# Two feed-forwards taken by pairs of sequences: up products over the 512 tokens of a pair, down products two inner tiles later

## What is computed

```
block 0:  x = x + proj(attention(film(rmsnorm(x))))          one head
          x = x + gelu_exact(film(rmsnorm(x)) @ w1 + b1) @ w2 + b2
block 1:  x = x + gate * proj(attention(modulate(ln(x))))    16 heads
          x = x + gate * (gelu_tanh(modulate(ln(x)) @ w1 + b1) @ w2 + b2)
w1: 256 x 1024     w2: 1024 x 256
```

## Time and profile before

| | |
|---|---|
| timed runs, median of 3 | 1631.18 us |
| profiled execution, first to last instruction (span) | 1626.9 us |
| PE busy | 1600.1 us (98%) |
| PE weight loads (PEld) busy | 1441.2 us (89%) |
| DVE / ACT / POOL busy | 1263.6 / 848.1 / 484.6 us |
| matmuls | 14558 |

### The profile page before, as it was taken

How to read it: one execution, slowest core, us unless ns; L and a number is a source line. 1 busy time by engine, 2 the same in 40 slices (tenths; PEclk the granted TensorE clock), 3 DMA queues, 4 the chain that set the end, 5 groups by cost and what they waited for, 6 DMA issues and landing times.

```text
span 1626.9 us, 42734 instructions
## 1 busy us (share of the span) xinstructions
PE 1600.1 (98%) x14558; PEld 1441.2 (89%) x14558; DVE 1263.6 (78%) x2892; ACT 848.1 (52%) x1696; POOL 484.6 (30%) x639
## 2 busy tenths in 40 slices
PE   8999999999999999999999999999998999999999
PEld 7999999999999998777777777777767999999999
DVE  5798887676666667788888888888885777777776
ACT  3666664333333344666776677767765333333332
POOL 2333331222121123243433344343424222222221
PEclk9999999999999999999999999999999999999999
DMA  6600001000000001332333333332331111111111
GB/s 177 208 20 22 20 16 54 5 1 1 0 0 0 0 2 41 108 111 96 107 103 112 102 103 105 104 109 98 109 116 35 40 44 49 39 52 39 39 52 39
DMA packets 103438, 100.68 MB, mean 62 GB/s; under 512 B 18672, under 2 KB 93872, under 8 KB 103360
## 3 DMA queue, kind: packets, MB, share of 16 engines
q1 hardware_dynamic: 103200, 99.61, 19.5%
q0 software_dynamic: 160, 0.04, 0.1%
HBM read 38.62 MB, written 8.55 MB: 29 GB/s over the span
## 4 chain that ended last, share of the span: by engine, by line
PE 94%; DVE 3%; ACT 1%; DMA 1%; issue 1%; SPq 0%; DVEq 0%; ACTq 0%
PE bank L207 66%; PE bank L1619 7%; PE bank L1601 7%; PE bank L1563 5%; PE bank L329 4%; PE bank L1629 2%; PE bank L1637 1%; PE bank L696 1%; PE bank L400 1%; PE bank L189 1%; PE bank L491 0%; DMA A_w_film<-in_L_cond_film_w 0%; DVE m_xhat L1575 0%; DVE C_negmax L1575 0%; DMA C_qs<-C_q_lo 0%
## 5 line engine op out<-in xcount | busy, mean ns | idle before, releaser
L1710 ACT ACTIVATE C_probs<-bank 128x1024 f32<-128x1024 f32 x256 | 262.6, 1026 | 154.6 <-PE bank L1601 154.3
L1575 DVE TENSOR_REDUCE C_negmax<-bank 128x4 f32<-128x1024 f32 x248 | 303.3, 1223 | 48.7 <-PE bank L1563 45.1
L983 ACT ACTIVATE B_g<-bank,B_bias 128x256 f32<-128x256 f32 x256 | 107.6, 472 | 210.8 <-PE bank L207 210.8
L983 ACT ACTIVATE D_g<-bank,D_bias 128x256 f32<-128x256 f32 x256 | 107.5, 472 | 210.4 <-PE bank L207 210.4
L296 POOL TENSOR_TENSOR m_rstd<-m_var,neghalf 128x2 f32<-128x2 f32 x64 | 52.2, 815 | 509.2 <-DVE m_var L287 259.6
L1601 PEld LDWEIGHTS bank<-C_qs,C_kx 64*128 64x128 f32 x1024 | 77.4, 185 | 79.4 <-ACT C_probs L1710 45.8
L207 PE MATMUL bank<-m_h_hi,B_wt_w_lo 128*128 128x256 f32 x512 | 147.5, 288 | 0.0
L207 PE MATMUL bank<-m_h_hi,D_wt_w_lo 128*128 128x256 f32 x512 | 146.9, 287 | 0.4 <-DVE m_h_lo L348 0.4
L207 PE MATMUL bank<-D_wt_w_hi,D_g_lo 128*128 128x256 f32 x512 | 145.7, 285 | 0.2
L207 PE MATMUL bank<-m_h_lo,B_wt_w_hi 128*128 128x256 f32 x512 | 144.8, 283 | 0.0
L207 PE MATMUL bank<-D_wt_w_lo,D_g_hi 128*128 128x256 f32 x512 | 144.6, 282 | 0.0
(11 more groups left out here) (257 smaller groups left out, 4994.9 us busy)
## 6 DMA issues: line engine op xcount, KB each, us to landing
C_qs<-C_q_hi SPq DMA_DIRECT2D x128, 128.0 KB
C_kx<-C_k_hi SPq DMA_DIRECT2D x128, 128.0 KB, 2.6
C_qs<-C_q_lo SPq DMA_DIRECT2D x64, 128.0 KB
C_kx<-C_k_lo SPq DMA_DIRECT2D x64, 128.0 KB, 2.1
C_gbc<-mod_rows SPq DMA_DIRECT2D x32, 256.0 KB, 3.4
D_gbc<-mod_rows SPq DMA_DIRECT2D x32, 256.0 KB, 3.3
out<-xres SPq DMA_DIRECT2D x31, 256.0 KB, 3.5
xres<-in_x SPq DMA_DIRECT2D x4, 1792.0 KB, 11.0
```

The lines of the kernel that those rows point to most:

```text
L983: ins = eng.activation(g[u][:, d * S:(d + 1) * S], hbank[u][:, d * S:(d + 1) * S], func, bias=per_seq(bias1, 2 * u + d, b))
L1575: e_max.by(eng.tensor_reduce(m4[:, :, :, j], spair[:, :].rearrange("p (e q k) -> p e q k", e=2, q=TH), AX, ALU.max, negate=True))
L1710: e_exp.by(eng.activation(probs[t % NP][:, :], stpair[:, :], ACT.Exp, scale=scl))
```

## The change

The feed-forwards run over pairs of sequences, 16 a phase.

- `up` takes one inner tile of 128 at a time, for both sequences of the pair: the moving operand is 512 columns wide. A tile is 2 x 3 = 6 matmuls of 512 columns, 8 tiles and 48 matmuls a pair. One tile fills one bank, and there are two banks for it (`H_TILE`).
- `gelu` and `split` of a tile have the sizes that they had for a group; there are 8 a pair, as 2 x 4 before. The split tiles are three buffers (`G_TILE`), the gelu outputs two, where there were four of each.
- `down` of a tile is 12 matmuls of 256 columns as before, for both sequences of the pair. It stands behind the up product of two tiles later.
- The transposes of the next pair stand behind tiles 1 and 4; both sequences of a pair must be normalized before its first up product.
- At the seams, the first pair's norms, up products 0 and 1 (B) or 0 to 3 (D), and down products 0 and 1 (D) are taken in the attention before. The gelus 0 and 1 of D get due times before those of the last exps. In iteration 1 of a feed-forward the tiles taken before are left out (`TAKEN`).
- At the end of D, the first sequence of the last pair has a residual of its own, ahead of the two halves of the last sequence.

```diff
...
+                G_TILE, H_TILE = (0, 1, 2, 0, 1, 2, 0, 1), (0, 1) * 4
...
+                TAKEN = NORMED | ({("up", u) for u in range(4)} | {("gelu", u) for u in range(4)} |
+                                  {("split", u) for u in range(4)} | {("down", 0), ("down", 1), ("xb", 0)} if l1 else
+                                  {("up", 0), ("up", 1), ("gelu", 0), ("gelu", 1), ("split", 0)})
...
+                def up(eng, m, u):
+                    if u == 0:
+                        norm.e_lo.wait(eng, m.seq(1))
+                    earlier(e_gelu, eng, m, u, last_use(H_TILE, u))
+                    e_mm1.by(mm3(eng, hbank[H_TILE[u]][:, :], [(w1.part(k, u * P, P), norm.pair_tokens(m, k)) for k in range(KT)]))
+
+                def down(eng, m, u):
...
+                    n = G_TILE[u]
+                    for s in range(2):
+                        for h in range(TH):
+                            c = slice(s * S + h * P, s * S + (h + 1) * P)
+                            ins = mm3(eng, out_half(m, s, h), [((g_hi[n][:, c], g_lo[n][:, c]), w2.part(u, 0, D))],
+                                      start=u == 0 and (h == 0 or final(m) and s == 1), stop=u == HT - 1, skip=True)
...
+                def gelu(eng, m, u):
+                    e_mm1.wait(eng, m, u + 1)
+                    earlier(e_glo, eng, m, u, 2)
...
+                def split(eng, m, u):
+                    n = G_TILE[u]
+                    e_gelu.wait(eng, m, u + 1)
+                    earlier(e_mm2, eng, m, u, last_use(G_TILE, u))
...
                 def tensor(eng):
+                    T_AFTER = {1: 0, 4: 1}
...
+                        for u in range(HT):
+                            if not taken("up", u, m):
+                                up(eng, m, u)
+                            q, d = (r, HT - 2 + u) if u < 2 else (m, u - 2)
+                            if not taken("down", d, q):
+                                down(eng, q, d)
+                            if u in T_AFTER and not taken("T", T_AFTER[u], f):
+                                b = f.seq(T_AFTER[u])
+                                norm.e_lo.wait(eng, b.back(1))
+                                norm.transpose(eng, b)
...
+                            if end == 0 and u == 2:
+                                heads["C"].head_k(eng)
...
+                            if end == 0 and u >= 5:
+                                heads["C"].head_scores(eng, u - 5)
...
                 def vector(eng):
...
+                        if not taken("stats", 0, f):
+                            norm.stats(eng, f.seq(0))
+                        for u in range(HT):
+                            if not taken("split", u, m):
+                                split(eng, m, u)
+                            if prep and i.reg is None and u in (0, 4):
+                                prep.vector(eng, 2 * i.off - 1 + u // 4)
...
+                            if u in (0, 2) and not taken("xhat", u // 2, f):
+                                norm.normalize(eng, f.seq(u // 2))
+                            if u == 1 and not taken("stats", 1, f):
+                                norm.stats(eng, f.seq(1))
+                            if u in (3, 5) and not taken("lo", u // 4, f):
+                                norm.evac_lo(eng, f.seq(u // 4))
+                            if u in (3, 4) and not taken("out", u - 3, r):
+                                residual(eng, r, u - 3)
...
-                NEXT_PE = {"B T": 536, "B up0": 549, "B up1": 555, "B down0": 556}
...
+                NEXT_PE = {"B T0": 527, "B T1": 541, "B up0": 550, "B up1": 557}
+                NEXT_ACT = {"B hi0": 530, "B hi1": 543, "B gelu0": 554, "B gelu1": 560}
+                NEXT_DVE = {"B stats0": 513, "B xhat0": 523, "B stats1": 525.5, "B lo0": 532.5, "B xhat1": 533.5, "B lo1": 546,
+                            "B split0": 558}
...
-                NEXT_PE = {"D T": 533, "D up0": 544.5, "D up1": 546.5, "D T1": 547.9, "D up2": 559.2, "D up3": 563.9,
-                           "D down0": 566, "D down1": 567, "D down2": 568}
-                NEXT_ACT = {"D hi": 545.8, "D w2 hi0": 546.6, "D w2 hi1": 548, "D w2 hi2": 550, "D w2 hi3": 553,
-                            "D hi1": 555.5, "D gelu0": 562.5, "D gelu1": 562.6, "D gelu2": 563.9, "D gelu3": 564}
...
+                NEXT_PE = {"D T": 533, "D T1": 542, "D up0": 547.7, "D up1": 550.5, "D up2": 553.5, "D up3": 556,
+                           "D down0": 566, "D down1": 568}
+                NEXT_ACT = {"D hi": 537, "D hi1": 546.5, "D w2 hi0": 546.6, "D w2 hi1": 548, "D w2 hi2": 550, "D w2 hi3": 553,
+                            "D gelu0": 551.6, "D gelu1": 552.3, "D gelu2": 562.7, "D gelu3": 563.9}
...
```

More of the change, by code:

```diff
@@ L996, in add_bias @@
[L996 to L1008 removed]
+                START, TAIL, PEELED = 1, 0 if l1 else 2, 2 if l1 else 6
@@ L1069, in it @@
                         f, m, r = i, i.back(1), i.back(2)
-                        last = i.off if not l1 and i.reg is None else None
+                        end = ending(i)
                         if l1 and i.reg is None and i.off in (START, START + 1):
-                            prev.e_res.wait(eng, Seq(None, NB - 3) if i.off == START else LAST)
-                        if f.exists(NB) and last != START:
-                            norm.stats(eng, f)
-                        if last != START:
-                            split(eng, m, 0)
@@ L1129, in it @@
+                        if end == 0:
                             heads["C"].norm.stats(eng, Seq(None, 2))
-                    run_pipeline(eng, NB, 2, it, START, TAIL)
+                    run_pipeline(eng, NPAIR, 2, it, START, TAIL, PEELED)
                 def gpsimd(eng):
                     def it(i):
-                        last = i.off if not l1 and i.reg is None else None
-                        if i.exists(NB) and last != START:
-                            norm.root(eng, i)
-                        if last == 1:
+                        f, m = i, i.back(1)
+                        end = ending(i)
+                        if not l1 and i.reg is None and i.off == START:
@@ L1149, in gpsimd @@
-                    run_pipeline(eng, NB, 2, it, START, TAIL)
+                        for s in range(2):
+                            if not taken("root", s, f):
+                                norm.root(eng, f.seq(s))
+                        for s in range(2):
+                            if not taken("xb", s, m):
+                                e_glo.wait(eng, m, 1 + 4 * s)
+                                add_bias(eng, m.seq(s))
+                            if prep and i.reg is None:
+                                n = 2 * i.off - 1 + s
+                                if prep.splits_weights(n):
+                                    e_glo.wait(eng, m, 2 + 4 * s)
+                                prep.gpsimd(eng, n)
+                            if end in (-1, 0) and s == 0:
+                                heads["C"].head_xhat(eng, end == 0)
@@ L1693, in tensor @@
                     scores(eng, FIRST, 4)
-                    prev.e_res.wait(eng, Seq(None, NB - 2))
+                    prev.norm.e_lo.wait(eng, LAST)
                     qk_cm(eng, SECOND, "q")
```

527 lines of the change are left out of this document (259 added, 268 removed).

## The result

The kernel became slower: 1657.53 us (median; 1656.58 to 1659.46) against 1630.61 us for the kernel before on the same chip. The ratio is 1.0173, 95% interval 1.0158 to 1.0187. I had forecast 1611, a gain of 1.2%. The profiled span is 1655.7 us, 28.8 us longer than that of the earlier trace rows.

A forecast was written before the change was run, and what follows sets the result against it. The prediction took PE's matmuls as the bound, idle only at seams. Up products -36.9 us and seams, preparation and clock +16.5 gave -20.4, so a 1606.5 us span and a 1611 us median; forecast range 1603 to 1620, with rivals 1599 to 1627.

The forecast's parts named there:

- What bounds the kernel now: Feed-forwards in mid-phase: PE waits for nobody, so time is matmul count times distance; idle PE time stands at seams only.
- What a 512-column matmul costs: Up products: 214 ns per 512-column matmul, bounds 213 to 238, against 119 ns per 256-column one before.
- Rival 1: Up products: the 12 ns surplus belongs to every matmul, so 225 ns, 16.9 us less gain, 1628 us; chance 0.11.
- rival 3: Up products: the distance grows with the columns, 238 ns, so the seams alone remain, 1648 us; chance 0.02.
- rivals 1 and 5: The fifth, up products: long matmuls overlap each other, 131 ns for 512 columns, 164 us gain, 1483 us; chance 0.01.
- Sum over the up products: Both feed-forwards: 48 matmuls at 214 ns replace 96 at 119, saving 1.15 us a pair, -36.9 us over 32 pairs.
- The new order keeps PE fed: Within each pair: all chains fit their slack, 0.4 us at the tightest, the first set of transposes; cost zero.
- rival 2: Step 1 of each pair: the transposes stall PE; a delay of 1.0 us a pair cancels the gain; chance 0.06.
- A to B: Start of B: PE waits about 4 us before sequence 2's transposes, and 1 us for up product 0; +5 us.
- B to C: End of B: `head_k`'s placing by DMA ends about 0.7 us late for C's first scores; +1 us.
- C to D: +7 us: less filler in C +2, end of C +0.5, a wait at D's start +4.2.
- Clock: Seams: new waits of 4 us may lower PE's granted clock; +1.5 us, bounds 0 and 3.5 for each.

The follow-up runs named there:

- e1: Trains of matmuls alone, the rest of the computation left out: fp32r of 512 columns 227.3 ns each, of 256 columns 119.7, bf16 of 512 columns 215.8.
- e5: Matmuls alone with feed-forward operands, six of 512 columns alternating with twelve of 256: 231.2 ns per 512-column matmul, against 227.3 in a row.
- e2: The changed kernel with each 512-column up product issued as two of 256 columns, nothing else changed: 1665.61 us, ratio 1.0228.
- e3: The changed kernel with gelus 0 and 1 of D, their splits and up products 2 and 3 behind C's last exps: 1649.13 us, ratio 1.0121.
- e9: The changed kernel with D's first low part and second xhat before C's last maxima on DVE, second low part earlier too: 1650.73 us, ratio 1.0143.

## Why the prediction was wrong

**What bounds the kernel now** was right for B and nearly so for D: in B the middle waits for nobody; in D, from 1354 us on, the kernel before has one wait of 0.2 us a pair for DVE's split, and its going gave 0.3 us a pair that stood in no term.

**What a 512-column matmul costs** is the first step that failed: "So 512 columns should take 512 / 2.4 = 213.3 ns; I take 214." It costs 233, of which 213.3 are columns, 14 a fixed price that comes with the fp32r format (e1), 4 the alternation with shorter ones (e5), and the rest is open. The reading that carried it, "where a matmul is longer than its weight load, nothing is added", came from rows of another format, and I read them wrongly: eight records of 427 ns for four matmuls, at half clock, and not 1024 cycles at full clock. The 12 ns above 106.7 that I had noted were the fixed price, in plain sight. Rival 1 (225 ns) had the mechanism and came within 2.3 ns of the bare train; in the kernel the distance is nearer to rival 3 (238). What I had against rivals 1 and 5, and in part against 3, was this same misread row.

**Sum over the up products**: -36.9 us was to be 32 x 1.15. Measured: 0.32 us a pair in B and 0.28 to 0.58 in D, about -11 us in the steady pairs. Of these the width, to which I had given all, brings 0.07 and 0.24 a pair, some 4 us (e2).

**The new order keeps PE fed**: right, in the middle. At steps 1 and 4 nothing waits; rival 2 did not happen.

**Seams.** *A to B*: the wait of 4 us was there to a tenth. Not foreseen: the low part of B's first sequence and the xhat of its second push A's last splits back on DVE, so that PE idles for 1.5 us before the attend products at 250.4; and the half clock. *B to C*: I took +1; it was a wait of 2.65 us at 611, with a half-clock stretch behind it. I had looked at `head_k`, and the wait was for `head_xhat`, which stands behind POOL's bias additions. *C to D* is the second step that failed: I took +7, of which 0.5 for the end of C "(bounds 0 and 5)". The end of C alone took 18 us more. I had priced the table loads (4 x 1.28) and not that each gelu stands between two exps, with a wait for PE on either side (e3: 8 us); nor had I checked the moved transposes against DVE's queue, where their xhat had not moved (e9: 5 to 7 us). *Tail*: +1.5 was right (1.6).

Of the 48 us between forecast and measured change (the span, less the 1.5 us at the start), the matmul's price and with it the gain of the pairs is 26, the seams with their half clock 22. With the seams as I had them and the pairs as measured the kernel would still have been 5 us slower; with the pairs as I had them and the seams as measured, 2 us slower. So either error alone was enough to turn the sign.

**Clock**: +1.5, bounds 3.5 for each new wait. At most 12 us, by the estimate above. The rows: 427 ns for 512 columns, and a granted clock of 0.93 and 0.86 in the windows. The rule of the Trainium skill ("TensorE: Matmul & The Clock Gate", "Why this matters for your kernels"), that idle gaps between bursts bring the half clock back, agrees with the stretches at waits of 3.7 to 4.7 us. It speaks of longer gaps than the waits of 1.75, 2.4 and 2.9 us that stood before three others (1246, 615 and 1260), and no wait of PE above 0.7 us stands before the one at 325. My term did not follow the rule. The page's 131 ns for 512 columns ("Back-to-back issue gap") is seen in no train here. Its other figure, columns by 2.4 and about 2.5 ns, agrees with the bf16 train (215.8) and not with fp32r (227.3).

*Preparation* and the 2 us of missing filler in C can't be told apart from the rest.

**Chances**: 0.10 for slower was too little. My own upper bounds, 225 ns (16.9 us), the end of C (4.5) and the clock (3.5 for each of six waits, 19.5 more than I took), together give 1652 us; I let them stand as separate, unlikely cases, though the last two have one cause, waits of PE at the seams.

## What to carry to other kernels

Take the price of a matmul from rows of the same number format and at the same clock, and count the records against the matmuls in the code before dividing. A fixed part in each one shows already as the distance above columns by clock, and a matmul twice as wide saves that part once. When an order is made coarser, write out for each moved instruction the queue of every engine that feeds it, at each end of a phase: here the middle gained 11 us and the ends lost 39, and a new order of the same instructions brought some 32 back (by the ratios). A wait of PE can cost more than its length: behind each of the longer ones in the changed kernel (2.4 to 4.7 us) some 3 to 5 us of PE's work ran at half clock.

## What I had not expected of the hardware

- At full clock fp32r matmuls have a fixed price of 13 to 14 ns, bf16 2.5 and each record of plain fp32 2.6 (e1). At half clock fp32r shows none: 427 ns for 512 columns.
- A plain fp32 matmul of 256 columns leaves two records of 216 ns at full clock, and of 427 at half clock.
- 32-column weights make a 512-column matmul slower (231.4 for 227.3 ns) and a 256-column one faster (113.6 for 119.7).
- Up products of 512 columns rise from 227.3 to 231.2 ns when they alternate with 256-column ones, with all other engines idle (e5). ACT at work adds nothing to that, and DVE and POOL at work add nothing either.
